# Reordering a hand-written schedule and moving a clamp from ScalarE to VectorE in a two-layer local-attention stage

## The reference

```python
def l2norm(t): return t / jnp.clip(jnp.linalg.norm(t, axis=-1, keepdims=True), 1e-12)
qkv = shift_token(x) @ wqkv                       # 8 heads of 64
q, k = l2norm(q) * qs, l2norm(k) * ksc
q, k = rotary_xpos(q, k)
sim = 8.0 * q_window @ k_window_and_the_one_before    # windows of 128 tokens
o = softmax(where(mask, -max, sim)) @ v
x = x + o @ wo
```

## Time and profile before

| | |
|---|---|
| median of 3 runs | 1997.19 us (1997.02 to 1997.55) |
| the profiled execution's own time | 1997.55 us |
| its span, first to last instruction | 1996.0 us |
| mean granted TensorE clock | 0.922 of full speed |
| busy over the span | PE 1787.4 us (90%), DVE 1109.8 us (56%), ACT 967.3 us (48%), POOL 934.7 us (47%) |
| first layer's local attention | from 549 us to about 1026 us |
| second layer's local attention | from about 1253 us to about 1732 us |
| one loop pass of it, 14 in all | 54.8 us |

### The profile page before, as it was taken

The page is one execution under the profiler, slowest core; times in us unless marked ns, Lnnn a source line. Parts: engine busy times, 40 slices in busy tenths (PEclk is TensorE's granted clock), DMA queues, the critical chain, the costliest instruction groups (busy, mean ns, idle before and its releaser), DMA issues. The chain is left out here.

```text
span 1996.0 us, 42845 instructions
## 1 busy us (share of the span) xinstructions
PE 1787.4 (90%) x14072; PEld 1353.2 (68%) x14072; DVE 1109.8 (56%) x2825; ACT 967.3 (48%) x1898; POOL 934.7 (47%) x923
## 2 busy tenths in 40 slices
PE   5899988898669999999979999599999999789887
PEld 3556655565347777777768888477777777577776
DVE  4566655666467766676523333676676666234343
ACT  2655545554336555555534444265555555333332
POOL 3355444554336655555423333455555555333433
PEclk7898888987779999999979999699999999799998
DMA  4333343334010000000121112100000001121221
GB/s 144 106 115 107 106 122 112 117 109 127 22 33 12 32 32 32 32 32 21 50 58 43 63 63 95 44 12 32 32 32 32 32 21 49 50 70 63 65 74 42
DMA packets 103736, 121.28 MB, mean 61 GB/s; under 512 B 23387, under 2 KB 75781, under 8 KB 103685
## 3 DMA queue, kind: packets, MB, share of 16 engines
q1 hardware_dynamic: 96772, 95.45, 15.7%
q0 software_dynamic: 6912, 25.17, 3.5%
HBM read 82.55 MB, written 37.77 MB: 60 GB/s over the span
## 5 line engine op out<-in xcount | busy, mean ns | idle before, releaser
L468 DVE TENSOR_REDUCE a_negm<-a_x 128x2 f32<-128x256 f32 (+3 forms) x256 | 202.4, 814 | 143.7 <-PE a_x L594 141.5
L430 ACT ACTIVATE a_PT<-a_c 128x384 f32<-128x384 f32 (+1 forms) x384 | 183.7, 522 | 139.7 <-PE a_c L633 84.4
L866 POOL TENSOR_TENSOR work<-work 128x512 f32<-128x512 f32 x128 | 164.5, 1287 | 152.2 <-DVE work L1016 151.0
L1541 DVE SCALAR_TENSOR_TENSOR m_hid<-m_a,mw_b,m_gate 128x512 f32<-128x512 f32 x96 | 71.9, 749 | 244.4 <-ACT m_gate L1479 219.8
L1034 DVE CUSTOM_DVE_ANT_0 l_x<-l_x,window 128x256 f32<-128x256 f32 (+1 forms) x512 | 184.1, 421 | 31.7 <-PE l_x L1131 31.7
L1065 PE MATMUL l_f<-w_hi,tails 128*128 128x512 f32 x384 | 168.8, 440 | 14.2 <-DVE work L1016 11.1
L949 ACT ACTIVATE l_PT<-l_c 128x512 f32<-128x512 f32 (+1 forms) x256 | 125.3, 542 | 87.8 <-PE l_c L1171 84.1
L1436 POOL TENSOR_TENSOR m_hid_lo<-m_hid,m_hid_hi 128x512 fp32r<-128x512 f32 x80 | 102.7, 1291 | 131.3 <-ACT m_hid_hi L1490 131.1
L1066 PE MATMUL l_f<-w_hi,tails 128*128 128x512 f32 x384 | 154.8, 403 | 0.0
L1067 PE MATMUL l_f<-w_lo,tails 128*128 128x512 f32 x384 | 154.1, 401 | 0.0
L880 POOL TENSOR_TENSOR l_PS<-l_PT 128x768 f32<-128x768 f32 x64 | 119.6, 1869 | 58.7 <-ACT l_PT L949 58.7
(11 more groups left out here) (240 smaller groups left out, 5091.8 us busy)
## 6 DMA issues: line engine op xcount, KB each, us to landing
a_Q<-qk_parts SPq DMA_DIRECT2D x192, 64.0 KB, 2.1
a_K<-qk_parts SPq DMA_DIRECT2D x192, 64.0 KB, 2.1
qk_parts<-a_qk_hi SPq DMA_DIRECT2D x32, 256.0 KB, 2.1
qk_parts<-a_qk_lo SPq DMA_DIRECT2D x32, 256.0 KB, 2.2
after_attn<-rows_out POOLq DMA_DIRECT2D x16, 512.0 KB, 5.2
xin<-after_attn SPq DMA_DIRECT2D x32, 256.0 KB, 3.1
m_xr<-after_attn SPq DMA_DIRECT2D x16, 512.0 KB, 4.1
xin<-in_L_attn_x SPq DMA_DIRECT2D x8, 512.0 KB, 3.5
```

The lines of the kernel that those rows point to most:

```text
L430: nc.scalar.activation(PT[:, p // PG % 2, 2 * (p % PG) + hh, QOFF[t]:QOFF[t] + nq], SC[hh][:, 0:nq], ACT.Exp, scale=AD ** -0.5).then_inc(e ...
L468: dve.tensor_reduce(negm[:, q, 2 * p:2 * p + 2], MX[i % 2][:, :, 0:nk], AX.X, ALU.max, negate=True).then_inc(max_done, 1)
L866: pool.tensor_tensor(t1[:, par, w, :], t1[:, par, w, :], t2[:, par, w, :], ALU.add)\
```

## The change

The change has two parts, both in `local_attention`, and so both layers have them.

First, the clamp under the inverse norm. Before, ACT did `f_iv` in three instructions: Relu of `ss` less 1e-24, Ln of that plus 1e-24, and Exp. After, DVE takes the maximum of `ss` and 1e-24 in a tensor_tensor of 128x16 inside each odd `f_qe` step, between the sum of squares and the rotary products. It waits first for its own sum of squares, and signals a new semaphore `ss_done`. ACT waits for that and does Ln and Exp alone.

Second, the list `STEPS` has a new order. Every step is still there.

```diff
-            f_x:0 f_xe:0 st:0 sm:4 f_qk:0 f_qe:0 st:1 f_qk:1 ps:0 f_qe:1 f_iv:0 f_qk:2 sm:5 f_qe:2 st:2 f_qk:3
-            f_qe:3 sm:6 pv:0 f_qk:4 f_iv:1 f_qe:4 f_qk:5 f_qe:5 sm:7 sv:0 z:0 st:3 f_qk:6 ps:1 f_iv:2 f_qe:6 zn:0
-            mt:1 f_qk:7 f_qe:7 st:4 f_iv:3 pv:1 st:5 ps:2 sv:1 z:1 st:6 zn:1 f_t:0 f_te:0 zs:0 pv:2 sv:2 f_sm:0
-            f_t:1 zs:1 z:2 f_te:1 st:7 zn:2 f_sm:1 f_t:2 pv:3 f_te:2 f_sm:2 ps:3 f_t:3 sv:3 f_te:3 f_sm:3 xr:0 zs:2
-            z:3 f_v:0 zn:3 zs:3 f_v:1 f_v:2 f_mt:0 f_v:3 out:0""".split()]
+            f_x:0 f_xe:0 sm:4 st:0 f_qk:0 sm:5 f_qe:0 st:1 ps:0 f_qk:1 f_qe:1 f_iv:0 sm:6 st:2 f_qk:2 pv:0 f_qk:3
+            f_qe:2 sv:0 f_qe:3 z:0 sm:7 st:3 ps:1 f_qk:4 f_iv:1 f_qe:4 f_qk:5 xr:0 mt:1 f_qe:5 f_iv:2 st:4 f_qk:6
+            f_qk:7 pv:1 zn:0 f_qe:6 f_qe:7 f_iv:3 st:5 sv:1 ps:2 z:1 st:6 pv:2 zn:1 zs:0 f_t:0 zs:1 f_te:0 sv:2
+            f_sm:0 z:2 f_t:1 zn:2 f_te:1 st:7 f_sm:1 f_t:2 f_te:2 ps:3 pv:3 zs:2 f_sm:2 f_t:3 sv:3 f_te:3 z:3 f_sm:3
+            f_v:0 zn:3 f_v:1 zs:3 f_v:2 f_mt:0 f_v:3 out:0""".split()]
...
-                pool.memset(least[:, 0:1], -1e-24).then_inc(least_set, 1)
-                pool.memset(least[:, 1:2], 1e-24).then_inc(least_set, 1)
...
-                act.wait_ge(least_set, 2)
...
-                        act.wait_ge(ss_raw, 2 * n + 2)
+                        act.wait_ge(ss_done, n + 1)
...
-                        nc.scalar.activation(inv[:, par, :], ss[:, par, :], ACT.Relu, bias=least[:, 0:1])\
-                            .then_inc(log_done, 1)
-                        act.wait_ge(log_done, 2 * n + 1)
-                        nc.scalar.activation(inv[:, par, :], inv[:, par, :], ACT.Ln, bias=least[:, 1:2])\
-                            .then_inc(log_done, 1)
-                        act.wait_ge(log_done, 2 * n + 2)
+                        nc.scalar.activation(inv[:, par, :], ss[:, par, :], ACT.Ln).then_inc(log_done, 1)
+                        act.wait_ge(log_done, n + 1)
...
+                    dve.memset(least[:, :], 1e-24).then_inc(least_set, 1)
...
+                    dve.wait_ge(least_set, 1)
...
+                        if w == 1:
+                            dve.wait_ge(ss_raw, b * 8 + i + 1)
+                            dve.tensor_tensor(ss[:, par, :], ss[:, par, :], least[:, :], ALU.max)\
+                                .then_inc(ss_done, 1)
```

More of the change, by code:

```diff
@@ L743, in local_attention @@
         sq = work[:, 2 * n_t + n_qk:2 * n_t + n_qk + 2 * INNER].rearrange("p (w n) -> p w n", w=2)
-        ss, inv, least = sb("ss", [P, 2, 2 * FH]), sb("inv", [P, 2, 2 * FH]), sb("least", [P, 2])
+        ss, inv, least = sb("ss", [P, 2, 2 * FH]), sb("inv", [P, 2, 2 * FH]), sb("least", [P, 2 * FH])
         QH, QL = sb("QH", [P, FH // 2, S + P], F32R), sb("QL", [P, FH // 2, S + P], F32R)
@@ L776, in local_attention @@
         front_free, v_done = sem("front_free"), sem("v_done")
-        sq_done, ss_raw = sem("sq_done"), sem("ss_raw")
+        sq_done, ss_raw, ss_done = sem("sq_done"), sem("ss_raw"), sem("ss_done")
         log_done, inv_done = sem("log_done"), sem("inv_done")
```

## The result

The changed kernel takes 2032.22 us (median, 2029.45 to 2034.21) against 1997.37 us (1997.02 to 1998.34) for the kernel before on the same chip. The ratio is 1.0168, with a 95% interval of 1.0155 to 1.0181. The profiled execution took 2031.94 us, with a span of 2030.5 us, which is 34.5 more than before. The forecast was 2023, its range 2008 to 2036. The measured time lies outside the 2017 to 2030 that the main theory was given, and inside the 2030 to 2037 of rival 3.

A forecast was written before the change was run, and what follows sets the result against it. PE alone was taken to bound the local attention. 1.75 us a pass over 14 passes gives 24.5, plus 0.6 for prologues and 0.6 for epilogues: 25.7 us on 1997.55, or 2023 us; range 2008 to 2036, with 2017 to 2030 likeliest.

The forecast's parts named there:

- the main theory: Local attention: PE bounds, and the new order's waits add 1.75 us a pass; 2017 to 2030 us, chance 0.6.
- rival 3: DVE becomes late too, with waits at `f_qk:2`, `f_qk:3` or `f_qk:7`: 0.5 to 1 us a pass, 2030 to 2037, chance 0.12.
- PE sets the time, and ACT's relief is worth nothing: Loop pass: PE busy 54.45 of 54.78 us, so ACT's 1.2 us a pass less work gains nothing.
- `mt:1`, then `st:4`: Now adjacent on PE: `st:4` waits for ACT's copy, 0.94 us lost; with gains, `pv:1` starts 0.1 us later.
- `st:6`, then `pv:2`: Now adjacent on PE: `pv:2` waits for `zn:1` to empty `OB`, cost 0.8 us a pass.
- `f_t:0`, `sv:2`, `f_sm:0`: `sv:2` alone covers the split of `f_te:0`: 0.5 us lost a pass, plus 0.2 for one more shape change.
- the upper bound: 2030 us: DVE's clamp at 0.53 us, and POOL possibly holding `sv:2`, 0.5 us a pass or 7 us.
- `f_t:2` held by 0.15 us: `zn:2` now precedes `f_te:1` on DVE, so `f_t:2` is held about 0.15 us a pass for its banks.
- rival 1: Faster: an emptier ACT delivers before PE asks, covering the bare pairs in the loop; 1988 us, chance 0.06.
- rival 2: Only the first two waits are real, the `f_te` chain is absorbed: 1.1 us a pass, 2014 us, chance 0.15.
- rival 4: Waits near 1 us lower the granted clock: 1 to 2 us a pass, 2040 us or more, chance 0.03.
- The clamp: DVE, odd `f_qe`: 0.29 us each, 0.17 to 0.53; nothing in the loop, 0.6 us for two prologues.

The follow-up runs named there:

- the order alone: The kernel before, Relu on ACT kept, with the new list `STEPS`: 2024.83 us, ratio 1.0131.
- the reduction in the new order: The changed kernel with the clamp as a tensor_reduce maximum over pairs of the sum and a preset 1e-24: 2026.53 us, ratio 1.0144.
- the clamp alone: The changed kernel, clamp on DVE, with the list `STEPS` of before: 2057.43 us, ratio 1.0296.
- scalar form: The changed kernel with the clamp as a tensor_scalar maximum with the constant 1e-24 in place of the tensor_tensor: 2030.06 us, ratio 1.0166.
- the new front: The kernel before with the new list up to `st:5` and its own list behind, `f_t:0` ahead of `pv:2`: 2015.96 us, ratio 1.0080.
- the reduction in the old order: The changed kernel with the list of before and the clamp as a tensor_reduce maximum over pairs: 2006.58 us, ratio 1.0039.

## Why the prediction was right, point by point

- **PE sets the time, and ACT's relief is worth nothing.** Right. ACT has 1.8 us less to do in a pass (the four Relus are 1.2 of it), and no experiment shows a gain from it.
- **`mt:1`, then `st:4`.** Right: 1.29 us between them, 1.35 forecast (the bracket is 0.69, where 0.9 was named), and the wait before `mt:1` is gone in the order alone and in the changed kernel.
- **`st:6`, then `pv:2`.** Right: 2.19 us in the order alone. In the changed kernel it is 1.98, only because `st:6` itself starts late. From `sv:1` to `pv:2` it is 3.21 us in both (683.88 to 687.09 with the order alone, 689.44 to 692.65 after), so that the chain of `z:1` and `zn:1` still sets it. The brackets name ACT or nothing, but `zn:1` ends 0.10 us before `pv:2` in both (686.99 and 692.55).
- **`f_t:0`, `sv:2`, `f_sm:0`.** Right in kind, 0.16 us short in size. Less the 0.06 us by which `st:4` came sooner, this is the difference between the 1.75 us forecast for a pass and the 1.82 to 1.87 of the order alone. In the changed kernel POOL holds `sv:2` for 0.42 us, as the upper bound feared, but this costs nothing more, since `f_sm:0` would have waited anyway.
- **`f_t:2` held by 0.15 us.** Right: its eight matmuls last 1.25 us instead of 1.09 in the order alone (1.26 in the changed kernel).
- **The rivals.** An emptier ACT did not deliver earlier (rival 1). All waits were real (rival 2). In the loop the clock stayed up (rival 4). DVE did not become the bound in the new order (rival 3), though in the changed kernel `f_qk:7` starts up to 0.40 us after the matmul before it instead of 0.23, in layer 1 alone. The time fell into rival 3's 2030 to 2037, but not by its 0.5 to 1 us a pass. The run that bears on rival 1 is the reduction in the new order. Over four passes of layer 1 its ACT is busy for 119.7 us, against 125.9 with the order alone, and PE's waits are the same. Rival 3 is told by the traces alone.
- **The clamp: the term that was mis-sized.** "I take 0.29 us", with 0.53 as the high bound. The start of the clamp was right (0.70 us after the sum's start at 687.37). Its length was not, up to 1.29 us and 1.53 in the clamp alone. The row that the price came from, a reciprocal of 128x16, is an instruction with no POOL work beside it, and as a price without the hold it was about right (0.22 in the reduction). The forecast had 0.6 us for all clamps. Against the order alone the two local attentions cost 3.6 us more (995.0 against 991.4). Of these, 1.8 lie in the two prologues up to `f_t:0` (32.58 us against 31.70, and 33.03 against 32.07), where 0.6 was forecast (behind `f_t:0` the two differ by 0.8 and by -0.7, which cancels), and some 1.0 in layer 1's passes. That is the late `f_qk:7`: in layer 1 the clamp of `f_qe:5` takes 0.48 to 0.54 us and `f_qk:7` loses 0.10 to 0.17, in layer 2 it takes 0.40 and `f_qk:7` loses nothing. The forecast had named just this place: nothing at 0.29, about 0.1 us a pass at 0.53. By medians the held clamp costs 8.1 us (34.9 against 26.7 over the kernels before), and 5.2 in its scalar form.

The Trainium skill (SBUF — State Buffer, "Who interferes with whom") says that a DVE instruction with two SBUF inputs, or one such as `tensor_scalar` in a two-port mode, contends with GpSimd for a shared pair of ports, that whichever starts first has it for its whole instruction, and that `tensor_reduce` on trn2 never contends. Our runs agree on the kinds: up to 1.29 us with two SBUF inputs, 0.19 in the reduction, and the scalar form was held up to 1.28, though no run shows which mode it ran in. They show one half of the order: POOL was always at work first, and the clamp then took until POOL's instruction ended. No clamp began first. The forecast did not use this rule, and it should have.

Why do clamps that are held for up to 1.29 us cost so little in the new order and 59 us in the old? In the old order DVE is at work without a pause up to `mt:1`, and each hold goes straight to PE: a pass is 58.58 us with the held clamps and 55.22 with the reduction. In the new order the delay reaches ACT (the Ln behind the clamp begins at 689.40, and so the exponentials that `st:6` needs are late) and POOL (`sv:2` waits for it). But both of these lie ahead of a longer wait. `pv:2` comes 3.21 us after `sv:1` in either case, and `f_sm:0` comes 2.75 us after `f_t:0`, against 2.74 in the order alone. So the waits of 0.15 and 0.42 us at `st:6` and `sv:2` are time that PE would have lost a step later anyway. In layer 2 a pass of the changed kernel is 56.54 us and one of the order alone 56.53.

**The sum.** Forecast 25.7 us, measured 34.5 between the two profiled spans: 1.3 more from the order in the two local attentions (26.4 with the order alone, 25.1 forecast for loop and epilogues), 3.0 more from the clamp, 3.4 in the first attention, 1.1 in the feed-forwards and the rest. The 3.4 us lie in code that is the same in both kernels. One stretch accounts for 3.8 us of difference, and it ran at a lower granted clock. The windows view of it, from the 1001st matmul of PE to the 1501st, before and after (granted clock third from the end):

```profile
95.95:158.37 62.42, 57.78 (x501) 37.56 (x501) 38.62 (x66) 34.60 (x72) 32.03 (x38) 0.86 0.38 114
```

```profile
95.96:162.14 66.18, 61.49 (x503) 38.58 (x501) 38.85 (x66) 34.73 (x72) 32.05 (x38) 0.78 0.35 105
```

PE is busy 3.7 us longer there, and the other engines are not. What lowers the clock isn't shown. In the ten profiles the first `f_x` starts between 547.6 and 552.3 us: at 552.3 in the changed kernel, 552.1 in the clamp alone, 550.2 in the kernel with `f_qk:6` moved, and 549.2 to 549.6 in the three other forms of the clamp, but also at 549.5 in the new front, which has the clamp of before. So nothing ties it to the change. It may be mere spread between executions; whether the others have it too, no trace shows. Of the 8.8 us that the forecast fell short, 4.3 are its own terms, the clamp and the order.

No version that was run beats the kernel before. The nearest, the reduction in the old order, is 0.4% slower.

## What to carry to other kernels

- In a hand-written order for queues that run in sequence, price a reorder by the pairs that become neighbours. If a consumer follows its producer with nothing between, look for a place in the same trace (a prologue or an epilogue) where that pair already stands bare: its distance is the price.
- A wait that is covered or removed moves to whatever is late next. Two halves of a reorder don't add up, since one can hide what the other exposes.
- The cost of a small instruction depends on what runs on the neighbour engine at that moment. Look for its duration beside work of that engine, in a row of the same kind of instruction and operands, before you move work to it.

## What was not expected of the hardware

- A DVE maximum of 128x16 between SBUF tiles took from 0.17 to 1.29 us (up to 1.54 in the clamp alone), always with a POOL instruction running when it began. It ended 0.03 to 0.04 us after one of POOL's did, in all 64. It took 0.17 us when POOL had 0.14 us to go; how long it takes with POOL idle, no run shows. The form with a constant behaved alike (0.17 to 1.28 us), and the reduction did not (0.185 to 0.189 us in all 64, with POOL at work at each start). The sums of squares, reductions too, took 0.63 to 0.69 us in all 128.
- DVE instructions that read one operand from PSUM showed no such hold. In the changed kernel the product on L1012, with a POOL instruction beside 112 of 128, took the same time throughout (ns: min, median, max):

```profile
L1012 DVE TENSOR_TENSOR work<-l_f,l_rots x128: 670/678/684, 562.2 to 1692.3; 128x512 f32<-128x512 f32 x128
```
